# Two pairs of VectorE operations change places in the attention loop of a gated cross-attention kernel

## The reference

```python
x = x + jnp.tanh(g_xattn[0]) * _L0_xattn_ref(_layernorm(x), ctx, ctx, Wq, bq, ..., Wo, bo)
#   qh = (q @ Wq.T + bq), kh, vh likewise, 16 heads of 32
#   attn = softmax(qh kh^T * 32**-0.5); out = attn @ vh; return out @ Wo.T + bo
x = x + jnp.tanh(g_ffn[0]) * _L0_ffn_ref(_layernorm(x), router_w, ...)
#   logits = xf @ router_w + router_b; the best 2 of 8 experts, gated, + 2 shared experts
x = x + jnp.tanh(g_xattn[1]) * _L1_xattn_ref(_layernorm(x), ctx)
x = x + jnp.tanh(g_ffn[1]) * _L1_ffn_ref(_layernorm(x), w1, conv_w, conv_b, w2)
```

## Time and profile before

| | |
|---|---|
| median of 3 runs | 1838.8 us (1838.42 to 1847.11) |
| the profiled execution, its time | 1847.11 us |
| its span in the profile | 1845.6 us |
| TensorE clock granted, mean of the span | 0.919 of full speed |
| attention's loop, full steps s = 2 to 14 | 126.20 to 447.81 us of the span |

### The profile page before, as it was taken

How to read it: one execution, slowest core, us unless ns; L and a number is a source line. 1 busy time by engine, 2 the same in 40 slices (tenths; PEclk the granted TensorE clock), 3 DMA queues, 4 the chain that set the end, 5 groups by cost and what they waited for, 6 DMA issues and landing times. The chain is left out here.

```text
span 1845.6 us, 26082 instructions
## 1 busy us (share of the span) xinstructions
PE 1603.4 (87%) x9190; PEld 1249.0 (68%) x9212; DVE 1089.4 (59%) x1834; ACT 779.1 (42%) x1393; POOL 588.0 (32%) x544
## 2 busy tenths in 40 slices
PE   7599999999489999999999999277657799999997
PEld 5488878877368788877788888254425666666664
DVE  3568888887543445422333333378866777777775
ACT  2144444444134222223344444145545665556753
POOL 0133333333134445633420000445403443234440
PEclk9699999999689999999999999656668899999998
DMA  3112222221398899835333333687721111111102
GB/s 128 46 58 92 82 91 92 75 86 66 143 331 296 293 322 341 291 100 178 138 110 106 108 108 108 202 295 254 257 109 53 47 46 69 69 69 69 43 4 92
DMA packets 108604, 252.38 MB, mean 137 GB/s; under 512 B 15411, under 2 KB 15411, under 8 KB 104296
## 3 DMA queue, kind: packets, MB, share of 16 engines
q1 hardware_dynamic: 65656, 121.98, 19.5%
q0 software_dynamic: 17056, 67.12, 10.1%
q10 hardware_dynamic: 25808, 62.14, 9.5%
HBM read 147.13 MB, written 101.97 MB: 135 GB/s over the span
## 5 line engine op out<-in xcount | busy, mean ns | idle before, releaser
L1223 PE MATMUL e_u_ps<-e_w,e_xeT 128*128 128x512 f32 x1596 | 395.3, 400 | 9.9 <-DVE e_xeT L1128 9.9
L1223 PEld LDWEIGHTS e_u_ps<-e_w,e_xeT 128*128 128x128 f32 x1596 | 294.5, 190 | 72.8 <-DVE e_w L1177 8.1
L1936 PE MATMUL b_f_ps<-b_xdT,w1q 128*128 128x512 f32 x1024 | 255.1, 405 | 11.5 <-DVE b_h L1841 9.6
L1936 PEld LDWEIGHTS b_f_ps<-b_xdT,w1q 128*128 128x128 f32 x1024 | 192.2, 191 | 65.2 <-DVE b_h L1841 18.4
L1774 POOL TENSOR_TENSOR b_h<-b_h,b_srow 128x512 f32<-128x512 f32 x112 | 143.7, 1326 | 244.9 <-ACT b_srow L1795 244.9
L1234 PE MATMUL e_y_ps<-e_w,e_hT 128*128 128x512 f32 x798 | 209.2, 404 | 3.9 <-DVE e_hT L1159 2.4
L1234 PEld LDWEIGHTS e_y_ps<-e_w,e_hT 128*128 128x128 f32 x798 | 142.6, 189 | 30.9 <-issue 4.0
L1802 ACT ACTIVATE b_h<-b_f_ps,cb,cw 128x512 f32<-128x512 f32 x128 | 105.0, 820 | 123.7 <-PE b_f_ps L1936 123.4
L1838 DVE SCALAR_TENSOR_TENSOR b_h<-b_f_ps,cw,b_h 128x511 f32<-128x511 f32 x128 | 95.8, 749 | 86.4 <-ACT b_h L1802 86.1
L452 POOL TENSOR_TENSOR prob<-prob,ri 128x1232 f32<-128x1232 f32 x32 | 74.5, 2327 | 128.2 <-DVE ri L547 128.2
L1913 PE MATMUL b_o_ps<-w2q,b_h 128*128 128x512 bf16 x446 | 106.0, 393 | 2.1 <-issue 1.1
(11 more groups left out here) (221 smaller groups left out, 2742.9 us busy)
## 6 DMA issues: line engine op xcount, KB each, us to landing
e_xe<-slots_in_scratch SPq DMA_DIRECT2D x69, 256.0 KB, 2.6
experts_out_scratch<-e_ye ACTq DMA_DIRECT2D x69, 256.0 KB, 2.0
xin<-in_x SPq DMA_DIRECT2D x16, 512.0 KB, 3.6
xres<-in_x SPq DMA_DIRECT2D x16, 512.0 KB, 3.7
x_scratch<-x SPq DMA_DIRECT2D x32, 256.0 KB, 2.1
xn_scratch<-xn SPq DMA_DIRECT2D x32, 256.0 KB, 2.1
e_xe<-xn_scratch SPq DMA_DIRECT2D x32, 256.0 KB, 4.4
e_fraw<-in_w1T ACTq DMA_DIRECT2D x8, 1024.0 KB, 7.9
```

Source lines behind the costliest of these rows:

```text
L1223: mm = pe.matmul(u_ps[:, i], xeT[:, pa, k], w[:, par, pb, k * 2 * HID:(k + 1) * 2 * HID], start=(k == 0 and (pa, pb) == PASSES[0]), stop=( ...
L1936: mm = pe.matmul(f_ps[:, u % RING], w1q[:, k, m * P:(m + 1) * P], xdT[:, part, k], start=(k == 0 and part == 0), stop=(k == KD - 1 and par ...
```

## The change

In VectorE's stream the two x2T copies (part "late") come after the two oT subtractions (part "back") and no longer before them. Nothing else is changed.

```diff
@@ in the run() of attention's VectorE stream @@
-                if late:
-                    for j in range(2):
-                        u = ("n", s - 2, j)
-                        dve.wait_ge(t_full, t_at[u] + 1)
-                        dve.tensor_copy(x2T[:, :, j * P:(j + 1) * P], quads(t_bank(*u))).then_inc(n_free, 1)
                 if back:
                     for i in range(2):
                         dve.wait_ge(o_hi, (s - 1) * 2 + i + 1)
                         dve.tensor_tensor(oT[:, 1, 2 * i:2 * i + 2],
                                           m_bank("o", s - 1, i).rearrange("p (a b) -> p a b", b=W2),
                                           oT[:, 0, 2 * i:2 * i + 2].bitcast(F32), ALU.subtract).then_inc(o_free, 1)
+                if late:
+                    for j in range(2):
+                        u = ("n", s - 2, j)
+                        dve.wait_ge(t_full, t_at[u] + 1)
+                        dve.tensor_copy(x2T[:, :, j * P:(j + 1) * P], quads(t_bank(*u))).then_inc(n_free, 1)
                 if mid:
                     softmax_sum(0)
```

## The result

The changed kernel takes 1873.61 us (median of 6 runs, 1865.45 to 1876.56) against 1838.61 (6 runs, 1837.97 to 1847.34). The ratio estimated from the runs is 1.0164, with a 95% interval of 1.0135 to 1.0194: 1.6% slower, 30 us. The plain medians differ by more, 35.0 us or 1.9%. By the ratio the time is 1868.8 us, inside my range of 1845 to 1870; the plain median lies 3.6 us above its end. I forecast 1858.5, so the direction was right and the loss too small.

A forecast was written before the change was run, and what follows sets the result against it. Each step was taken as bound by VectorE from the scores to the first x1, then TensorE from "l" to the next scores. Waits 9.9 plus clock 9.8 gave 19.7 us on 1838.8: 1858.5 us, range 1845 to 1870.

The forecast's parts named there:

- oT comes before its input: VectorE in full steps: oT must wait for ScalarE's high part, so VectorE loses 0.44 us up to the first x1.
- x2T late, "x" waits: TensorE in full steps: "x" transposes wait for banks the later x2T copies free, a pause of about 1.4 us.
- The slack ahead of "l" takes 0.85, 0.67 is left: TensorE, full steps: "w" starts 1.52 us later, slack before "l" absorbs 0.85; 0.67 us over 13 steps is 8.7 us.
- The clock falls, 1.5 us each time: TensorE in full steps: the new pause behind the scores can lower the granted clock, 1.5 us a time, landing in "w".
- It falls in half of the 13 steps, 9.8 us: Full steps s = 2 to 14: clock falls in the middle number of them, 6.5 x 1.5 = 9.8 us.
- The rival in which the clock stays: Full steps: clock holds at 1.00 and only the waits cost, 1848.7 us; chance 0.24.
- s = 15 and s = 16, 1.2 us: End of attention: s = 15 loses 1.7 us as "r" and "w" move later, s = 16 wins 0.5 us.
- Not slower, because the slack takes the delay: Full steps: with the high part 0.44 us sooner, 0.23 us a step remains, 1843.0 us; chance 0.12.
- Nearly all steps fall, 1870.8 us, at 0.10: Full steps: the clock falls in nearly every one, 13 x 1.7 us on top of the waits; chance 0.10.
- faster, at 0.04: TensorE in full steps: earlier oT lets "w" start sooner, at most 13 x 0.11 = 1.4 us gained; chance 0.04.
- My likeliest case: Full steps: the clock falls in some of them, 3 to 10, giving 1853 to 1864 us; chance 0.50.

The follow-up runs named there:

- ohi_early: Changed kernel with ScalarE's copy of oT's high part moved between the two halves of exps(0): 1858.77 us, ratio to before 1.0087.
- fill_full: Changed kernel with 12 more full-array "n" transposes in each full step, filling TensorE's wait for x2T: 1855.01 us, ratio to before 1.0072.
- fill_scores: Changed kernel with the last scores matmuls of scores(1) repeated in full steps, 12 more, filling the pause with weak work: 1859.18 us, ratio to before 1.0091.
- step_longer: Changed kernel with the last "p" transposes of each full step done four times, far from the pause: 1881.73 us, ratio to before 1.0219.
- x1_first_swapped: Changed kernel with the first x1 taken ahead of the two xT subtractions on VectorE: 1867.14 us, ratio to before 1.0147.
- alternate: Changed kernel with the new order only in odd steps and the old order in even ones: 1855.54 us, ratio to before 1.0071.

## Why the prediction was right in kind and too small

- *oT comes before its input.* Forecast: 0.44 us lost by VectorE. The trace has 0.36 idle, with oT at 264.72 and 1.36 us behind the start of xn, where x2T now stands at 0.91: 0.45 later. ohi_early took it away and got back 0.45 us a step (25.44 to 24.99). Right.
- *x2T late, "x" waits.* Forecast a pause of 1.4 us; it is 1.55 us. Right in place, a little short.
- *The slack ahead of "l" takes 0.85, 0.67 is left.* Measured 0.70 in each step without a fall, 9.1 us over 13 steps in fill_full against the 8.7 forecast. Right.
- *The clock falls, 1.5 us each time.* Measured 26.95 - 25.44 = 1.5 us. fill_full shows it to be a cause of its own. The rival in which the clock stays, which I gave 0.24, is out. The clock fell at pauses of 1.55 us, and in fill_scores behind a wait of 0.21 us. All of these are shorter than what the Trainium skill warns of (page "TensorE: Matmul & The Clock Gate", section "Why this matters for your kernels"): for this loop the measurement decides against reading that rule as a bound below which the clock is safe.
- *It falls in half of the 13 steps, 9.8 us.* This is the term that was mis-sized: 11 falls in the profiled execution, 16.5 us. I had taken the middle between no step and all of them. What I did not ask is how one step's fall bears on the next. The trace shows it in the place of the fall within the step, counted from VectorE's first maximum of the scores:

```profile
233.29:241.00 7.71, 6.16 (x94) 4.58 (x94) 7.28 (x11) 2.98 (x6) 2.28 (x2) 1.00 0.21 70
241.00:244.40 3.40, 3.40 (x14) 2.18 (x10) 3.30 (x6) 1.66 (x4) 2.25 (x1) 0.50 0.00 0
...
285.71:292.20 6.49, 4.94 (x83) 3.65 (x79) 6.06 (x10) 2.41 (x4) 2.17 (x2) 1.00 0.19 40
292.20:295.60 3.40, 3.40 (x17) 2.21 (x18) 3.33 (x5) 1.58 (x3) 1.25 (x1) 0.50 0.23 84
```

  In the first five steps the fall comes 6.0, 6.6, 7.0, 7.4 and 7.7 us behind the start, since the falls are 27.3 us apart and the steps mostly 26.9 to 27.0. The sixth has none and takes 25.44 us, and from the seventh on it is 6.5, 6.9, 7.3, 7.6 and 8.0, and then none again. So a fall makes its step nearly as long as the time to the next fall and carries the next pause into it. In all six kernels with falls, 43 falls in all, each begins 5.9 to 8.0 us behind its step's start, where the wait for x2T ends at 6.0 to 6.5 us. In one kernel the steps with a fall and those without have the same work and the same pause; they differ in the moment. step_longer, with 28.0 us a fallen step, had 6 of 13, as forecast; x1_first_swapped 10, as forecast; alternate 4 of 6; ohi_early, 26.5 us and a pause of 1.1 us, 8 of 13. Why the falls come 27.3 us apart no run here shows. And 11 is not the number of every execution: of eight on record the profiled one was the slowest, with a mean granted clock of 0.906, and two took 1865.45 and 1865.67 us at 0.914 and 0.913. How many falls those have no profile shows.
- *s = 15 and s = 16, 1.2 us.* Measured 4.2, the other term that was too small. "r" in s = 15 stands 479.87 - 472.79 = 7.08 us behind the step's start, 5.19 before: 1.89 later, forecast 1.86. The rest goes with the clock, 0.73 in this stretch in place of 0.77, which I had not priced there; a fall of its own begins right there, while "r" and "w" run:

```profile
479.87 1.06 PE L677 MATMUL m_ps<-x2T,rw 128*32 128x256 f32 x8 [2.15 <-DVE x2T L577]
480.85 6.99 PE L686 MATMUL m_ps<-wo,oT 128*128 128x512 f32 x24
```

  With the swap still in it, the end of attention took 48.7 us in fill_full and 47.4 in fill_scores, so 4.2 us is not a price of the waits.
- *Not slower, because the slack takes the delay.* Its condition was tried in ohi_early: 0.25 us a step is what remains then, as its 0.23. Falls stayed all the same, in eight of 13 steps.
- *Nearly all steps fall, 1870.8 us, at 0.10; faster, at 0.04.* The first came closest in its mechanism, with 11 of 13. Of the second nothing was seen: "w" starts 268.41 - 267.84 = 0.57 us behind "r" in place of 0.68, the 0.11 us that I allowed it, and "x" stands in front of both.

In sum: 18.5 us forecast for the full steps and 25.4 measured, 1.2 and 4.2 for the end. My likeliest case, 3 to 10 falls and 1853 to 1864 us, was missed on both counts, and that the time still lies in the range, by the ratio and not by the median, is partly luck. The 30.0 us are those of the two profiled executions; where the other 5.0 us between the medians arise is not known.

## What to carry to other kernels

A copy that frees a buffer is worth its place in the stream by all who wait for it, those who need the buffer as well as those who read the copy: in a full step the "x" transposes, which only need x2T's bank, stood first in line and waited 1.55 us, and in s = 15, where there are none, x2T's reader "r" waited 2.15 us. Before a wait is put into TensorE's stream, look at what stands on both sides of it, since a pause can cost more through the clock than through the waits: here 1.5 us each time it fell, against 0.7 of waits in the step. Filling it with repeated work gave the 1.5 us back. When such a cost depends on timing, ask also whether a step with the cost leads the next one into it; the average over all positions, which I took, gave 9.8 us where 16.5 were measured.

## What was not expected of the hardware

- The granted clock fell to 0.50 behind 3.40 us in which TensorE was busy 3.31 us, nearly all of it scores in 32-row tiles (56 records, 77 columns each). The busy time of the profile alone doesn't tell whether the clock will hold.
- Repeated work made a kernel faster: 156 transposes more, 16.3 us less in the full steps and 18.6 us less at the median (1855.01 against 1873.61).
- The number of falls changed from 11 to 6 of 13 with 12 transposes put into another part of the step, the pause of 1.55 us and the rows around it being the same.
